# The last feed-forward step of a two-layer transformer block: statistics from half products, reordered silu, four PSUM banks and one output batch on GpSimd

## The reference, cut to what matters

```
xn = layernorm(x)
s  = attention(xn)
y  = xn
for l in range(2):
    y = y + window_attention(shift(y)) @ wo
    h = shift(y);  mu, var = mean(h), var(h)          # over the 256 features
    h = (h - mu) / sqrt(var + 1e-5) * ln_g + ln_b
    a, g = split(h @ w1 + b1)
    y = y + (a * gelu(g)) @ w2 + b2
out = x + s * silu(y)
```

## Time and profile before

| | us |
|---|---|
| median of three runs | 1428.98 |
| the profiled execution, whole | 1429.2 |
| its span (first to last instruction) | 1427.3 |
| PE busy in the span | 1374.4 (96%) |
| DVE busy | 967.2 (68%) |
| ACT busy | 876.4 (61%) |
| GpSimd (POOL) busy | 763.8 (54%) |
| the last step, from the end of the last attention to the end of the span | 1377.0 to 1427.3 |

### The profile page before, as it was taken

One profiled execution on the slowest core, in us unless ns is written; L12 is line 12 of the kernel. 1 busy time (PEld: TensorE's weight loads), 2 busy tenths in 40 slices (PEclk: granted clock), 3 DMA queues, 4 the chain that ended last, 5 costly groups with the idle time before them and its releaser, 6 DMA issues.

```text
span 1427.3 us, 24111 instructions
## 1 busy us (share of the span) xinstructions
PE 1374.4 (96%) x7740; PEld 1050.6 (74%) x7740; DVE 967.2 (68%) x2671; ACT 876.4 (61%) x2223; POOL 763.8 (54%) x522
## 2 busy tenths in 40 slices
PE   6999997999999999999999999999999999999987
PEld 5777775777777777777777767777777777777766
DVE  5878667767666666666666777676767676766657
ACT  3556656475757574747576676656575757574764
POOL 2335767373737382837374746565564747373710
PEclk9999999999999999999999999999999999999998
DMA  7011100000000000000001010000000000000036
GB/s 219 30 59 56 59 30 1 0 1 0 0 0 0 0 0 0 0 0 0 0 1 59 2 60 1 1 0 0 0 0 0 0 0 0 0 0 0 0 128 226
DMA packets 35243, 33.33 MB, mean 23 GB/s; under 512 B 8364, under 2 KB 32896, under 8 KB 35200
## 3 DMA queue, kind: packets, MB, share of 16 engines
q1 hardware_dynamic: 35200, 32.79, 7.2%
HBM read 24.39 MB, written 8.39 MB: 23 GB/s over the span
## 4 chain that ended last, share of the span: by engine, by line
PE 77%; ACT 11%; DVE 5%; issue 4%; POOL 2%; DMA 0%; ACTq 0%; SPq 0%; DVEq 0%; POOLq 0%
PE l_psF L1394 9%; PE l_psP L837 9%; PE l_ring L837 9%; PE l_ring L1394 8%; PE l_ring L1464 7%; ACT l_att L1068 7%; PE l_psP L1448 6%; PE l_psF L1482 6%; PE l_psS L1405 5%; PE l_psS L1417 4%; PE l_ring L648 3%; PE l_psF L1434 2%; PE l_psP L683 1%; PE l_psS L666 1%; ACT L1158 1%
## 5 line engine op out<-in xcount | busy, mean ns | idle before, releaser
L950 POOL TENSOR_TENSOR l_att<-l_att 128x1024 f32<-128x1024 f32 x64 | 153.1, 2403 | 318.0 <-DVE l_att L875 318.0
L1002 POOL TENSOR_TENSOR l_att<-l_att,l_rinv 128x1024 f32<-128x1024 f32 x64 | 126.6, 1978 | 70.3 <-DVE l_rinv L1238 69.7
L1048 ACT ACTIVATE l_att<-l_psP 128x384 f32<-128x384 f32 (+1 forms) x128 | 70.2, 548 | 121.1 <-PE l_psP L1448 120.6
L1243 DVE COPY l_att<-l_psP 128x384 f32<-128x384 f32 (+1 forms) x128 | 78.8, 616 | 86.7 <-PE l_psP L1448 83.6
L1448 PE MATMUL l_psP<-ident,l_att 128*128 128x128 f32 x896 | 124.8, 280 | 2.0 <-DVE l_att L1243 1.5
L1448 PEld LDWEIGHTS l_psP<-ident,l_att 128*128 128x128 f32 x896 | 98.9, 141 | 32.4 <-issue 28.2
L957 POOL TENSOR_TENSOR l_att<-l_att,l_rn 128x1024 f32<-128x1024 f32 x64 | 120.9, 1910 | 0.7 <-ACT l_rn L856 0.5
L1068 ACT ACTIVATE l_att<-l_psF,l_nb 128x256 f32<-128x256 f32 x256 | 117.8, 482 | 2.1 <-DVE l_nb L1231 2.1
L966 POOL TENSOR_TENSOR l_u_lo<-l_att,l_u_hi 128x512 fp32r<-128x512 f32 x75 | 96.0, 1292 | 39.0 <-ACT l_u_hi L1043 38.7
L1464 PE MATMUL l_ring<-l_att 128*64 128x256 f32 (+1 forms) x1024 | 112.3, 362 | 2.0 <-ACT l_att L1048 1.4
L1231 DVE CUSTOM_DVE_ANT_0 l_psF<-l_psF,w_mask 128x256 f32<-128x256 f32 x256 | 101.0, 454 | 16.4 <-issue 16.4
(11 more groups left out here) (209 smaller groups left out, 4039.6 us busy)
## 6 DMA issues: line engine op xcount, KB each, us to landing
a_tables<-in_x SPq DMA_DIRECT2D x8, 512.0 KB, 4.3
scratch_s<-a_o SPq DMA_DIRECT2D x8, 512.0 KB, 3.2
l_att<-in_x SPq DMA_DIRECT2D x8, 512.0 KB, 8.6
l_att<-scratch_s SPq DMA_DIRECT2D x8, 512.0 KB, 8.9
out_dram<-l_att SPq DMA_DIRECT2D x7, 512.0 KB, 7.8
aw_stage<-in_wqkv SPq DMA_DIRECT2D x2, 768.0 KB, 6.1
l_att<-in_wqkv SPq DMA_DIRECT2D x2, 768.0 KB, 5.7
w_w_raw<-in_w SPq DMA_DIRECT2D x2, 640.0 KB
```

The source lines that it names most:

```text
L950: pool.tensor_tensor(rot[:, t, :], rot[:, t, :], t2[t % 2], ALU.add).then_inc(S["added"], 1)
L1002: pool.tensor_tensor(pr, pr, along(inv, 2 * P), ALU.mult).then_inc(S["p_done"], 1)
```

## The change

1. Mean: PE multiplies both halves of the features as they are finished (`x_attn`) by the matrix of 1/256 and adds up in PSUM, in place of one product of DVE's sum. Variance: ACT squares each half by itself, PE adds up two products, DVE's `sum_squares` is gone.
2. ACT runs six `silu` (before: nine) ahead of the squares.
3. `ln_g` and `ln_b` are applied by DVE (`tensor_scalar` with one scalar per partition, 128x512 twice) in place of ACT's four instructions; ACT only copies to the high part.
4. `y_of` has four banks in place of two; `turned_back(10)` to `(13)` stand between the `hidden` groups 2, 3 and 4; the second half of `down` waits for `silu_done` 12, since it shares a bank.
5. Batch 6 is combined by GpSimd (semaphores `prod_side`, `sum_side`).
6. DVE waits for all eight `xs_in` at one place, ahead of `combine(0)`; `combine` itself no longer waits for them. The order of `combine` on DVE is changed.

```
-    y_of = (psP[:, N:2 * N], psS[:, N:2 * N])
+    y_of = (psP[:, N:2 * N], psS[:, N:2 * N], psP[:, 0:N], psS[:, 0:N])
...
 sync
-            ge(sp, S["sum_done"], b + 1)
+            if b == B - 2:
+                sp.wait_ge(S["sum_side"], 1)
+            else:
+                ge(sp, S["sum_done"], b + 1 - (b == B - 1))
...
 gpsimd
+            if not attn:
+                pool.wait_ge(xs_in[B - 2], 32)
+                ge(pool, S["silu_done"], KD * (B - 1))
+                g, x, s = last_parts(B - 2, slice(0, KD))
+                pool.tensor_tensor(g, g, s, ALU.mult).then_inc(S["prod_side"], 1)
+                pool.wait_ge(S["prod_side"], 1)
+                pool.tensor_tensor(x, g, x, ALU.add).then_inc(S["sum_side"], 1)
...
 scalar
-                for n in range(9):
+                for n in range(6):
                     silu(n)
-                square()
-                silu(9)
+                ge(act, S["d_done"], i)
+                for k in range(KD):
+                    act.activation(sqF[:, k, :], dF[:, k], ACT.Square).then_inc(S["sq_end"], 1)
                 act.preload_act_table_set(NLE)
                 inverse_deviation()
                 act.preload_act_table_set(SILU)
-                high_f()
-                for k in range(KD):
-                    affine(k)
-                for n in range(10, 14):
+                ge(act, S["hn_done"], i)
+                act.activation(fhi[:, :, :], dF, ACT.Copy).then_inc(S["f_hi"], 1)
+                for n in range(6, 10):
                     silu(n)
...
-                for n in range(14, 2 * B):
+                for n in range(10, 2 * B):
                     silu(n)
...
 vector
                 less_mean()
+                for b in range(B):
+                    dve.wait_ge(xs_in[b], 32)
                 combine(0)
-                sum_squares()
+                ge(dve, S["rstdF_done"], i)
+                for k in range(KD):
+                    dve.tensor_tensor(dF[:, k], dF[:, k], psF[:, 0:N], ALU.mult).then_inc(S["scaled"], 1)
+                for k in range(KD):
+                    dve.wait_ge(S["scaled"], k + 1)
+                    last = dve.tensor_scalar(dF[:, k], dF[:, k], W.gcol[:, lf, k:k + 1], W.bcol[:, lf, k:k + 1], ALU.mult, ALU.add)
+                last.then_inc(S["hn_done"], 1)
+                ge(dve, S["f_hi"], i)
+                dve.tensor_tensor(flo[:, :, :], dF, fhi[:, :, :].bitcast(F32), ALU.subtract).then_inc(S["f_lo"], 1)
                 combine(1)
...
 tensor
                 for j in range(HT):
                     hidden(i, j, attn)
-                ge(pe, S["x_attn"], KD * i)
+                    if 2 <= j < 4:
+                        turned_back(2 * j + 6)
+                        turned_back(2 * j + 7)
                 down(i, 0, range(HT))
+                ge(pe, S["silu_done"], 12)
                 down(i, 1, range(0, 3))
```

More of the change, by code:

```diff
@@ L802, in layers_programs @@
              "pT_sb0 pT_sb1 o_ps o_hi o_lo wo_ps x_attn h_sum mean_ps d_done sqF_done sq_sum var_ps lnF_done rstdF_done hn_done affine_done "
-             "f_hi f_lo w1_ps gelu_done u_done u_hi u_lo u_lo_last w2_ps x_ffn y_ps silu_done prod_done sum_done out_done").split()
+             "f_hi f_lo w1_ps gelu_done u_done u_hi u_lo u_lo_last w2_ps x_ffn y_ps silu_done prod_done sum_done prod_side sum_side mean_end sq_end scaled out_done").split()
     S = {n: sem(n) for n in names}
@@ L886, in turned_of, with last_parts @@
         return psF if attn_alone and t % 2 else psS
+    def last_parts(b, few):
+        g = xT[:, b, 0:2 * X1].rearrange("p (k c) -> p k c", k=KD)[:, few, 0:N].rearrange("p k (t d) -> p k t d", t=TT)
+        x, s = (xs[:, j, b].rearrange("p t (k d) -> p k t d", k=KD)[:, few] for j in range(2))
+        return g, x, s
     def first_high(act):
@@ L1052, in silu @@
             ge(act, S["y_ps"], n + 1)
-            act.activation(xT[:, b, c * X1:c * X1 + N], y_of[n % 2], ACT.Silu).then_inc(S["silu_done"], 1)
+            act.activation(xT[:, b, c * X1:c * X1 + N], y_of[n % 4], ACT.Silu).then_inc(S["silu_done"], 1)
         def o_evac(i, pair):
@@ L1213, in combine @@
         def combine(b, few=slice(0, KD)):
-            n = b + few.start + 1
+            n = b + few.start + 1 - (b == B - 1)
             ge(dve, S["silu_done"], KD * b + few.stop)
-            ge(dve, xs_in[b], 32)
-            g = xT[:, b, 0:2 * X1].rearrange("p (k c) -> p k c", k=KD)[:, few, 0:N].rearrange("p k (t d) -> p k t d", t=TT)
-            x, s = (xs[:, j, b].rearrange("p t (k d) -> p k t d", k=KD)[:, few] for j in range(2))
+            g, x, s = last_parts(b, few)
             dve.tensor_tensor(g, g, s, ALU.mult).then_inc(S["prod_done"], 1)
@@ L1471, in turned_back @@
             ge(pe, S["x_ffn"], KD * (B + b) + (c + 1 if b == B - 1 else KD))
-            ge(pe, S["silu_done"], n - 1)
+            ge(pe, S["silu_done"], n - 3)
             for t in range(TT):
-                last = pe.transpose(y_of[n % 2][:, t * P:(t + 1) * P], xT[:, b, c * X1 + t * P:c * X1 + (t + 1) * P], ident[:, :])
+                last = pe.transpose(y_of[n % 4][:, t * P:(t + 1) * P], xT[:, b, c * X1 + t * P:c * X1 + (t + 1) * P], ident[:, :])
             last.then_inc(S["y_ps"], 1)
@@ L1490, in step @@
             if not attn:
-                for n in range(4):
+                for n in range(2):
                     turned_back(n)
-                mean(i)
-                for n in range(4, 10):
-                    turned_back(n)
-                variance(i)
-                for n in range(10, 14):
+                for k in range(KD):
+                    ge(pe, S["x_attn"], KD * (i - 1) + k + 1)
+                    last = pe.matmul(psF[:, 0:N], ones[:, :], xT[:, B - 1, k * (X1 - 1):k * (X1 - 1) + N], start=(k == 0), stop=(k == KD - 1))
+                last.then_inc(S["mean_ps"], 1)
+                for n in range(2, 6):
+                    turned_back(n)
+                for k in range(KD):
+                    ge(pe, S["sq_end"], k + 1)
+                    last = pe.matmul(psF[:, N:2 * N], ones[:, :], sqF[:, k, :], start=(k == 0), stop=(k == KD - 1))
+                last.then_inc(S["var_ps"], 1)
+                for n in range(6, 10):
                     turned_back(n)
```

15 lines of the change are left out of this document (5 added, 10 removed).

## The result

The changed kernel takes 1450.31 us (median of four runs, 1448.38 to 1453.05), the kernel before 1429.47 us in the same comparison (four runs, 1427.89 to 1430.09). The ratio is 1.0146, with an interval of 1.013 to 1.0161: 1.5% slower, 20.8 us. The forecast was 1451.5 us, with a range of 1445.3 to 1453.5. The profiled execution took 1450.83 us; its span is 1449.0 us against 1427.3 before, so 21.7 us more.

What follows compares the result with a forecast made beforehand. PE bounds the kernel, except in the last step, where the last batch's FFN chain holds hidden. 14.7 + 1.3 + 1.8 - 0.4 + 4.7 + 0.4 = 22.5 us on 1429.2, less 0.2: 1451.5 us, range 1445.3 to 1453.5.

Steps and rivals of the forecast that it cites:

- The wait for all loads: Before combine(0) on DVE: the last load's landing holds DVE until 1404.3; hidden starts at 1410.1, +14.7 us including the following chain.
- The chain behind it: From combine(0) to hidden: combine, two PSUM products, two tensor_scalar (1.0 us) and ACT's copy, from 1404.3 to 1410.1.
- What is bought ahead is worth nothing: Between 1377 and 1388 us: half products, dropped sum_squares, fewer silu and four banks are hidden by the wait.
- rival "faster": At combine(0): the wait costs nothing and the shorter front gains; 1426.8 us, or 1431 with GpSimd's full price; chance 4%.
- PE's clock: First hidden group: after idling, PE runs 4.2 us at half clock, so the group takes 4.9 us, +1.3 us.
- The transposes between the groups: turned_back(10) to (13) now lie on PE behind hidden 2 and 3: four groups at 0.45 us, +1.8 us.
- First half of `down`: On PE: 4.2 us instead of 4.62, as no combine stands ahead of the last two gated; -0.4 us.
- GpSimd beside DVE: Between the two add_ffn: two-SBUF-operand instructions of both engines go one after another, 9.3 us instead of 4.63, +4.7 us.
- The last transposes: On PE ahead of the end: about 5 us of idling before turned_back(15) slows four transposes, +0.4 us.
- rival "wait without GpSimd's price": Between the two add_ffn: GpSimd's batch costs DVE little and PE's second half of down decides; 1446.9 us, chance 24%.
- three things that could have made it slower still: Longer low clock in hidden, hidden 2 to 4 waiting for DVE, or late last output: 1453.5 to 1455 us, chance 8%.
- PE's wait for `silu_done` 12: Ahead of the second half of down: can hold PE some tenths, but does not show behind GpSimd's term.

Runs made afterwards that it cites:

- batch 6 on DVE: Changed kernel with batch 6 combined by VectorE again, behind combine(5), the wait for all loads kept: 1449.65 us, ratio 1.0138.
- split waits: Changed kernel with the eight load waits put back into the single combines, each waiting for its own batch: 1428.87 us, ratio 0.9997.

## Why the prediction was right, point by point

**The wait for all loads.** Forecast: DVE resumes at 1404.3, with a load as releaser, and `hidden` starts at 1410.1, +14.7 us. Measured: 1405.01 and 1410.75, +15.3 us. Of the 0.6 us too few, 0.33 are that this execution reached its last step later (1377.49 against 1377.16), the rest is that the load landed at 1404.79 and DVE took 0.22 us from there to its first row, not the 0.07 of the earlier trace rows. The chain shows steps of DVE's queue in these 0.22 us, and they are the same 0.22 with batch 6 on DVE and in the kernel before with the one wait; that they are the price of eight waits in place of one is likely, but was not tested. The chain behind it came out as summed: 5.74 us from `combine(0)` to `hidden` (forecast 5.8), the two `tensor_scalar` at 1.00 us, the value taken between 0.8 and 1.4. What fixed this price was the landing of the last load in the trace of before, and it had not moved.

**What is bought ahead is worth nothing.** Right for the changed kernel: DVE was through with `less_mean` at 1381.6, and the wait for the loads hid all else. How large the gain behind it was I had only as a side term of the rival "faster": front another 1 us. It is 2.6 us (split waits). With it, that rival would have been at 1429.4 with GpSimd's full price in place of 1431, and 1428.87 was measured.

**PE's clock.** Forecast 4.9 us for `hidden` 0, +1.3; measured 4.21 us (1410.75 to 1414.96), +0.6. The step that was mis-sized is "I take 4.2 us at half clock, between the two": by the widths of the rows it ended after some 2.7 us, less than in both rows it was taken from. That PE had idled 24 us in place of 4.56 did not make it longer. The size is also partly chance: with batch 6 on DVE, the same code after the same idleness took 4.50 us.

**The transposes between the groups.** +1.8 forecast; two pairs at 0.88 us in the chain, so 1.8. **First half of `down`:** 4.2 us as forecast, but the reason given was half wrong: a `combine` does stand ahead of `gated(4)`, the last but one (`combine(4)`, 1426.42 to 1428.90). It held nothing, because the transposes between the groups had made PE, and with it ACT's `gelu`, late enough: `gelu` 4 ended at 1428.80. Sum to `add_ffn(0)`: +17.4 forecast, 1433.71 - 1416.41 = 17.3 measured; the clock's 0.7 too many and the landing's 0.6 too few cancel.

**GpSimd beside DVE.** The mechanism is as forecast, row by row. GpSimd's product starts at 1435.17 while DVE's runs to 1435.6, and ends at 1437.84; DVE's sum, issued at 1435.62, ends 1.08 us after that, at 1438.92; GpSimd's sum, issued at 1437.92, ends 1441.13, that is 2.2 us after DVE's; and DVE's next one, issued at 1438.85, ends 0.54 us after that. They take turns, one instruction each. The Trainium skill (SBUF — State Buffer, "Who interferes with whom") calls the shared pair of ports an exclusive lock, and has issue order decide who blocks; by that rule the term was 4.7 us, and the trace agrees in kind. Measured are 8.60 us between the two `add_ffn` against the forecast 9.3, so +4.0. Two sizes were off. "GpSimd's product 2.40" comes from a row of another sum with other operands; here, free of waiting, both instructions take 2.2 us, 0.3 us less together. And a DVE instruction that was kept out ends 1.08 or 0.54 us after it is let in, not 1.22 or 0.69, 0.3 us less together: some of its fixed time seems to pass while it waits. With the split waits it is 1.07 and 0.54, in the kernel before with batch 6 on GpSimd 1.09 and 0.55; the reason was not tested. The earlier trace rows had it already: GpSimd's product ends at 47.81 and DVE's sum at 48.36, 0.55 us later, not the 0.69 read there.

**The last transposes.** 0.4 us forecast, and 1.11 us in place of 0.66 measured; from `add_ffn(1)` to the end of the span 6.69 in place of 6.26.

Sum: 14.7 + 1.3 + 1.8 - 0.4 + 4.7 + 0.4 = 22.5 forecast; 15.3 + 0.6 + 1.8 - 0.4 + 4.0 + 0.4 = 21.7 measured, which is the difference of the spans. So the mechanisms held, and what was too much or too little in their sizes was within 0.7 us each and of both signs; that the sum came out within 0.8 us is in part luck. The lower end of the range was added up wrongly (1446.9 - 0.8 - 0.5 is 1445.6, not 1445.3), which changes nothing here. The rival "wait without GpSimd's price", 1446.9 us, fell by the rows of GpSimd and by the run with batch 6 on DVE. None of the three things that could have made it slower still came: the clock was back within `hidden` 0, no `hidden` group waited for DVE, and SP issued the last output at 1446.34, right behind the last sum. PE's wait for `silu_done` 12 did come (0.43 us ahead of the second half of `down`), and was hidden by DVE's longer chain, as forecast.

## What to carry to other kernels

A wait stands for everything behind it on its engine. Before waits for loads are gathered at one place, look up in the trace when the last of them lands and which critical work is queued behind: here one line that moved up cost 21 us, and the improvements it stood in front of (5.7 us by the start of `hidden`) could not be seen until it was gone. In these traces work given to GpSimd, with operands in SBUF, takes its time from VectorE as long as VectorE's instructions read two SBUF tiles too; so give it some where VectorE has slack, and not just ahead of the step that all else waits for.

## What the runs showed that I had not expected

- How long PE stays at half clock did not follow how long it had idled. After 23.7 us of idleness `hidden` 0 took 4.21 us once and 4.50 us once, after 2.99 us (split waits) 4.45, all against 2.91 at full clock. The last four transposes took 1.11 us after 2.29 us of idleness (batch 6 on DVE) and after 4.12 us (the changed kernel), but 0.73 us after 4.13 us in the kernel whose PE was kept busy before.
- Filling PE with matmuls that nobody reads is a way to measure the clock's price alone: 1.3 to 1.6 us for a group of twelve matmuls 128x512.
- What GpSimd takes from DVE is a little less than its own time: two GpSimd instructions of 2.2 us each stretched DVE's rows by 4.2 us in the changed kernel. In the middle of the FFN it was 3.6 us, since there an instruction that reads only one tile from SBUF ran beside them unhindered.
- The same code ahead of 1377 us takes up to 4.5 us more or less from one execution to the next, which is more than most terms of this study; the tail, measured from one and the same event, can tell terms of 1 us apart with one trace each.
